# Third last gate-and-up selection made one down product sooner; token tiles of the last down products take turns over the banks

## The reference, cut to what matters

```python
xn = layernorm(x)                                   # 2048 tokens x 512
x = x + attn(xn, qkv, o_proj, gamma, beta) + ffn(xn, w_gate, w_up, w_down)

def ffn(x, w_gate, w_up, w_down):                   # hidden width 2048
    h = silu(x @ w_gate) * (x @ w_up)
    g = h.reshape(B, S, I // 4, 4)                  # of each four neighbours
    _, idx = top_k(abs(g), 2)                       # the two largest stay
    h_sparse = (g * mask(idx)).reshape(B, S, I)
    return h_sparse @ w_down
```

## Time and profile before

| | |
|---|---|
| median of 3 runs | 839.53 us |
| the profiled execution, its own time | 840.95 us |
| its span, first to last instruction | 839.2 us |
| TensorE busy, 3635 matmuls | 813.9 us, 97% |
| VectorE busy | 578.6 us, 69% |
| ScalarE busy | 314.1 us, 37% |
| mean granted TensorE clock | 0.992 |

### The profile page before, as it was taken

The page is one execution under the profiler, slowest core; times in us unless marked ns, Lnnn a source line. Parts: engine busy times, 40 slices in busy tenths (PEclk is TensorE's granted clock), DMA queues, the critical chain, the costliest instruction groups (busy, mean ns, idle before and its releaser), DMA issues.

```text
span 839.2 us, 9524 instructions
## 1 busy us (share of the span) xinstructions
PE 813.9 (97%) x3635; PEld 664.7 (79%) x3635; DVE 578.6 (69%) x985; ACT 314.1 (37%) x514; POOL 13.3 (2%) x33
## 2 busy tenths in 40 slices
PE   7998999999999999999999999998999999999997
PEld 5786887888888888887788788787888888888875
DVE  6856675445623347869988889699559568567796
ACT  5524133111511125554527436264234233323531
POOL 2100100000000000000000000000000000000000
PEclk9999999999999999999999999999999999999999
DMA  9511341240110208366534544871557262151002
GB/s 331 174 73 64 125 139 42 72 125 26 51 36 23 69 25 351 132 257 236 216 116 169 217 161 157 341 283 33 205 191 242 119 226 107 68 226 51 1 0 101
DMA packets 30012, 117.03 MB, mean 139 GB/s; under 512 B 2912, under 2 KB 2960, under 8 KB 27536
## 3 DMA queue, kind: packets, MB, share of 16 engines
q1 hardware_dynamic: 25792, 108.83, 35.0%
q10 hardware_dynamic: 4176, 7.60, 2.8%
HBM read 74.45 MB, written 41.97 MB: 139 GB/s over the span
## 4 chain that ended last, share of the span: by engine, by line
PE 72%; DVE 12%; ACT 5%; issue 3%; DVEq 0%
PE bank L481 10%; PE bank L483 10%; PE bank L482 9%; PE bank L605 9%; PE bank L607 9%; PE bank L606 9%; PE bank L687 5%; PE bank L689 5%; PE bank L688 5%; ACT mag L806 3%; PE bank L523 2%; DVE hs_lo L1153 1%; DVE wset L922 1%; DVE g_sum L1094 1%; ACT bank L802 1%
## 5 line engine op out<-in xcount | busy, mean ns | idle before, releaser
L605 PE MATMUL bank<-X_hi,wset 128*128 128x512 f32 x448 | 176.5, 394 | 3.5 <-DVE g_sum L1094 2.9
L606 PE MATMUL bank<-X_lo,wset 128*128 128x512 f32 x448 | 175.1, 391 | 0.0
L607 PE MATMUL bank<-X_hi,wset 128*128 128x512 f32 x448 | 175.1, 391 | 0.0
L605 PEld LDWEIGHTS bank<-X_hi,wset 128*128 128x128 f32 x448 | 84.5, 189 | 27.0 <-ACT bank L802 5.6
L607 PEld LDWEIGHTS bank<-X_hi,wset 128*128 128x128 f32 x448 | 84.4, 188 | 17.6
L606 PEld LDWEIGHTS bank<-X_lo,wset 128*128 128x128 f32 x448 | 84.5, 189 | 17.1
L687 PE MATMUL bank<-dw,hs_hi 128*128 128x512 f32 x224 | 87.9, 392 | 2.1 <-DVE acc L1118 1.6
L688 PE MATMUL bank<-dw,hs_hi 128*128 128x512 f32 x224 | 87.2, 389 | 0.0
L689 PE MATMUL bank<-dw,hs_lo 128*128 128x512 f32 x224 | 87.2, 389 | 0.0
L1118 DVE TENSOR_TENSOR acc<-bank,acc 128x512 f32<-128x512 f32 x64 | 43.4, 687 | 51.5 <-PE bank L689 51.5
L481 PE MATMUL bank<-xT_hi,zg_hi 128*128 128x512 f32 (+3 forms) x160 | 59.4, 371 | 0.1
(11 more groups left out here) (165 smaller groups left out, 1409.9 us busy)
## 6 DMA issues: line engine op xcount, KB each, us to landing
w_operands<-wset SPq DMA_DIRECT2D x8, 3584.0 KB, 11.8
wset<-w_operands SPq DMA_DIRECT2D x8, 3584.0 KB, 11.9
wsum<-w_units SPq DMA_DIRECT2D x28, 256.0 KB, 3.6
dw_raw<-L_ffn_w_down SPq DMA_DIRECT2D x14, 512.0 KB, 4.9
xw<-L_attn_x SPq DMA_DIRECT2D x4, 1024.0 KB, 9.6
xt_raw<-x_t SPq DMA_DIRECT2D x8, 512.0 KB, 7.2
xn_t<-xt_raw SPq DMA_DIRECT2D x8, 512.0 KB, 5.1
X_raw<-xn_t SPq DMA_DIRECT2D x8, 512.0 KB, 4.9
```

The source lines that it names most:

```text
L605: pe.matmul(dst[:], u[:, 0, :], x_hi, start=(first and kt == 0), stop=False, skip_group_check=True)
L606: pe.matmul(dst[:], u[:, 0, :], x_lo, start=False, stop=False, skip_group_check=True)
L607: last = pe.matmul(dst[:], u[:, 1, :], x_hi, start=False, stop=(kt == 1), skip_group_check=True)
```

## The change

It does four things.

1. Half 13 is selected in step 14, behind the selection of half 12, with its magnitudes in memory of its own (`mag_apart`, 144 KB, inside `wset0`, so after `gate_up(14)`). VectorE's comparisons and keeps for it stand between the four `add_down` of half 12. ScalarE makes its high parts in step 15, ahead of the last `down_hi` (conversion of down weights) and of two magnitudes of half 14.
2. Down products 13 and 14 add up in the same banks (6, 7, 2, 3); both belong to the same output tiles. `add_down(13)` is gone: four VectorE adds fewer. Half 15 takes banks (0, 1, 4, 5).
3. Down product 14 goes through r outside and the four token tiles inside; down product 15 does so for tiles (0, 1), then (2, 3).
4. On VectorE nothing stands any longer between the low parts of half 14 and the comparisons of half 15. The last gate and up sums are added ahead of the selection of half 14, and the last multiplication stands inside it. The remaining eight adds all come last.

The core of the diff:

```diff
+        mag_apart = at("mag_apart", 144 * KB, [P, G, W], F32)
-            return mag if i < ND - 2 else last_mag[i - (ND - 2)]
+            return mag if i < ND - 3 else mag_apart if i == ND - 3 else last_mag[i - (ND - 2)]
-            return bank[((6, 7, 2, 3), (0, 1, 4, 5), (6, 7, 2, 3))[i - (ND - 3)][t] ...
+            return bank[((6, 7, 2, 3), (6, 7, 2, 3), (0, 1, 4, 5))[i - (ND - 3)][t] ...
 # TensorE
+                pe.matmul(dst, s_hi, d_h, start=(r == 0 and i != ND - 2), stop=False)
+            def down_by_hidden(i, some):
+                for t in some:
+                    bank_free(i, t)
+                for r in range(G):
+                    if 0 in some:
+                        hidden_wait(i, r)
+                    for t in some:
+                        down_part(i, t, r)
+                if 2 <= n < N_Q:
+                    down(n - 2)
+                elif n == N_Q:
+                    down_by_hidden(ND - 2, range(TC))
+                elif n > N_Q:
+                    down_by_hidden(ND - 1, (0, 1))
+                    down_by_hidden(ND - 1, (2, 3))
 # ScalarE, step 15 behind the snapshots of P6
                 elif n == N_Q - 1:
+                    kept_hi(i)
                     down_hi(ND // 2 - 1)
+                    magnitude(ND - 2, 0)
+                    magnitude(ND - 2, 1)
 # ScalarE, end of step 14
+                if n == N_Q - 2:
+                    act.wait_ge(full[1], FILLS * (n + 1))
+                    for r in range(G):
+                        magnitude(ND - 3, r)
 # VectorE, end of step 14
+                elif n == N_Q - 2:
+                    add_down(i, 0)
+                    first_beats(i + 1)
+                    last_beats(i + 1)
+                    add_down(i, 1)
+                    count_beats(i + 1)
+                    add_down(i, 2)
+                    keep(i + 1, 0)
+                    keep(i + 1, 1)
+                    add_down(i, 3)
+                    keep(i + 1, 2)
+                    keep(i + 1, 3)
```

More of the change, by code:

```diff
@@ L306, in down_bank, with added_no @@
         def down_bank(i, t):
-            return bank[((6, 7, 2, 3), (0, 1, 4, 5), (6, 7, 2, 3))[i - (ND - 3)][t] if i >= ND - 3 else 6 + (TC * i + t) % 2]
+            return bank[((6, 7, 2, 3), (6, 7, 2, 3), (0, 1, 4, 5))[i - (ND - 3)][t] if i >= ND - 3 else 6 + (TC * i + t) % 2]
+        def added_no(i, t):
+            return TC * (i if i < ND - 2 else i - 1) + t + 1
         def a_free(n):
@@ L438, in _ @@
                         tile = (down_half[d] % 2) * TC + t
-                        sp.wait_ge(added, TC * d + t + 1)
+                        sp.wait_ge(added, added_no(d, t))
                         sp.dma_start(out_tiles[(d // NQ) * 2 * TC + tile], acc[:, tile, :]).then_inc(out_stored, 16)
@@ L665, in bank_free @@
                         pe.wait_ge(hid_ready, 4 * last + 1)
-                elif i == ND - 2:
+                elif i == ND - 1:
                     if t == 0:
@@ L672, in bank_free, with down_part, hidden_wait @@
                         pe.wait_ge(summed[t - 2], 2 * last + 2)
-                else:
-                    pe.wait_ge(added, TC * (ND - 3) + t + 1)
+            def down_part(i, t, r):
+                s_hi, s_lo = hs_hi_at(i)[:, r, t * P:(t + 1) * P], hs_lo_at(i)[r][:, t * P:(t + 1) * P]
+                d_h, d_l = dw_at(i // 2)[:, r // 2, 0, r % 2, :], dw_at(i // 2)[:, r // 2, 1, r % 2, :]
+                dst = down_bank(i, t)[:]
+                pe.matmul(dst, s_hi, d_h, start=(r == 0 and i != ND - 2), stop=False)
+                pe.matmul(dst, s_hi, d_l, start=False, stop=False)
+                last = pe.matmul(dst, s_lo, d_h, start=False, stop=(r == G - 1 and i != ND - 3))
+                if r == G - 1:
+                    last.then_inc(down_full, 1)
+            def hidden_wait(i, r):
+                pe.wait_ge(hs_ready, G * i + r + 1)
+                if i % 2 == 0 and r % 2 == 0:
+                    pe.wait_ge(dw_ready, i + r // 2 + 1)
             def down(i):
@@ L678, in down @@
                     bank_free(i, t)
-                    dst = down_bank(i, t)[:]
                     for r in range(G):
                         if t == 0:
[L682 to L690, removed]
+                            hidden_wait(i, r)
[5 more added lines that the diff above has]
+                    if 0 in some:
+                        hidden_wait(i, r)
+                    for t in some:
+                        down_part(i, t, r)
             for n in range(N_Q + 2):
@@ L808, in kept_hi @@
             def kept_hi(i):
+                if i == ND - 3:
+                    act.wait_ge(down_full, TC * i)
                 for r in range(G):
@@ L834, in _ @@
                 else:
-                    if i >= 0:
+                    if i >= 0 and n < N_Q - 1:
                         magnitudes(i)
@@ L866, in _ @@
                 nc.scalar.activation(g_sum[3][:], bank[0][:], ACT.Silu).then_inc(silu_ready, 1)
-                if n < N_Q - 1:
-                    last_silu(n)
+                if n == N_Q - 1:
+                    act.wait_ge(hid_ready, 4 * n + 2)
+                    magnitude(ND - 2, 3)
+                    act.wait_ge(hid_ready, 4 * n + 3)
+                    magnitude(ND - 2, 2)
+                last_silu(n)
                 if n == 2:
@@ L885, in _ @@
                 magnitude(ND - 1, r)
-            kept_hi(ND - 2)
-            last_silu(N_Q - 1)
             act.wait_ge(hid_ready, 4 * N_Q)
             magnitude(ND - 1, G - 1)
+            kept_hi(ND - 2)
             kept_hi(ND - 1)
@@ L1114, in add_down @@
                     dve.wait_ge(acc_loaded, 16 * (i // NQ + 1))
-                if i == ND - 2:
-                    dve.wait_ge(added, no - TC + 1)
                 dve.wait_ge(down_full, no + 1)
@@ L1163, in _ @@
                 i = n - 2
-                picks = i >= 0
+                picks = 0 <= i < ND - 3
                 if picks:
@@ L1184, in _ @@
                 elif n == N_Q - 1:
+                    for r in range(G):
+                        kept_lo(i, r)
                     down_lo(ND // 2 - 1)
@@ L1236, in _, with keep_all @@
                     add_down(i, 3)
-                elif picks and n < N_Q - 1:
+                elif n == N_Q - 2:
[10 more added lines that the diff above has]
+                    keep(i + 1, 3)
+                elif picks:
                     for t in range(TC):
                         add_down(i, t)
-            i = ND - 3
+            def keep_all(i):
+                keep(i, 0)
+                for r in range(1, G):
+                    keep(i, r)
+                    kept_lo(i, r - 1)
+                kept_lo(i, G - 1)
+            n, i = N_Q - 1, ND - 2
+            add_sum(0, n, bank[4], F_P4, g_sum[1], 3)
+            add_sum(1, n, bank[5], F_P4, a_tile(n, 1), 3)
+            first_beats(i)
+            last_beats(i)
+            hidden(n, 4, 2, g_sum[1], a_tile(n, 1))
+            count_beats(i)
+            keep_all(i)
+            dve.wait_ge(picked, G * (i + 1))
             first_beats(i + 1)
@@ L1245, in _ @@
             count_beats(i + 1)
[L1246 to L1268, removed]
+            keep_all(i + 1)
+            for i in (ND - 2, ND - 1):
+                for t in range(TC):
+                    add_down(i, t)
 INPUTS = ["L0_attn_x", "x_t", "L0_attn_qkv", "L0_attn_o_proj", "L0_attn_gamma", "L0_attn_beta",
```

9 lines of the change are left out of this document (removed).

## The result

The changed kernel takes 834.82 us (median of 8 runs, 834.42 to 836.92), the kernel before 839.42 us (8 runs, 838.1 to 841.58). The ratio is 0.9946, 95% interval 0.9933 to 0.9958: 4.6 us faster. The forecast was 835.6, range 834.1 to 838.4.

The account below looks back on a forecast made before the run. TensorE bounds the kernel, losing 5.87 us at the end, mostly waiting for VectorE's low parts and at low clock. New losses of 1.70 replace these: 4.17 gained, less 0.25, gives 3.9 us and 835.6 us, range 834.1 to 838.4.

Parts of the forecast that it names:

- (a): Step 14, bank 7: TensorE waits for VectorE's add of token tile 1, behind four comparisons; loss 0.65 us.
- (b): Step 15, first copies: the wait behind four magnitudes on ScalarE goes; gain 0.34 us.
- (c): Step 15, P5 copy: new instructions ahead of it on ScalarE make TensorE wait; loss 1.06 us.
- (d): From gate_up(15)'s end to product 15: product 14 without a gap, half 15's first low part slightly late; 0.33 us lost.
- (e): Clock at the new stalls (0.5, 0.9, 0.2 us): too short to bring the low clock, no cost.
- (f): Taking turns over banks in the last products: cost taken as 0, bounds 0 to 0.3 us.
- The rival on turns: Products 14 and 15: turns over four banks bring the clock down, making the kernel slower, up to 845 us; chance 0.06.
- (g): Kernel's end: last products of half 15 fill 0.68 us apart, so stores crowd; cost 0.25 us, bounds 0 to 0.4.
- the 3.19: VectorE work from 810.84 to 814.03, five instructions between the last two selections, leaving the path: 3.19 us.

Follow-up runs that it names:

- e6: Changed kernel with five VectorE additions (3.0 us) put between the low parts of half 14 and the comparisons of half 15; tail 72.25 us against 67.81.
- e2: Changed kernel with VectorE's add of token tile 1 in step 14 behind two comparisons of half 13, not four; tail 67.14 us against 67.81, median 835.66 us.
- e1: Changed kernel with ScalarE's two magnitudes of half 14 behind the P5 copies in step 15, not ahead; tail 66.71 us against 67.81, median 835.53 us.
- e5: Kernel before with only the turns over token tiles in products 14 and 15 put in; tail 72.98 us against 72.1.

## Why the prediction was right

*What bounds.* That 5.87 us were lost in the tail, and that they hung on the path VectorE - low part - TensorE, held: with three microseconds of VectorE's work put back between the selections (e6), TensorE idled 2.93 us ahead of product 15, the low clock was back, and the tail was 4.44 longer. That it came to 72.25, near the 72.1 of the kernel before, is in part chance: e6 has the new waits, the turns and the shared banks, which that kernel has not.

*(a), (b), (c).* 0.67, 0 and 1.07 us measured for 0.65, 0 and 1.06. e2 and e1 remove (a) and (c) by moving the one or two instructions that the prediction named, and give back 0.67 and 1.10.

*(d).* Half 15's comparisons were to begin 811.86 - 798.69 = 13.17 us after gate_up(15), and began 13.05 after it. The wait and restart ahead of product 15 were 0.21 instead of 0.33.

*(e), (f).* No low clock after waits of 0.34 and 0.74 us. In products 13 and 14 there is no late start at all: 21.76 us from 796.55, 0.2267 apart with turns over four banks as without (the 0.08 us ahead of product 15, at 818.39, are in (d)). The rival on turns finds nothing here. The rule of the Trainium skill that was set beside it (TensorE: Matmul & The Clock Gate, section "A second HAM failure mode: psum-queue depth-cycling") tells of a kernel that idled between its groups of matmuls; this one cycles through banks without idling, and the granted clock is 1.00 from 796 to 830 us.

*(g), the term that was off.* The end was to cost 0.25 us more and cost 0.07 less. Two stores 0.68 us apart landed in 2.0 us each; the 2.4 of the earlier trace rows was of the last two of five stores in a row, each 0.6 us behind the other, which landed in 2.1 us (the first) to 2.5 us (the last). With 0.12 from (d), that is the difference between 3.9 and 4.3 us. The rest of the 4.6 between the medians is scatter: the repeat gave 2.7 (839.3 against 836.61). So it is partly luck that the median, too, came within 0.8 us of the forecast.

*What it did not see.* It gave the shared banks no term of their own, though 1.1 us of the 4.3 are theirs (the two adds were counted inside the 3.19). And it took the turns as independent of where the last sums stand, which e5 refuted. In the change itself neither matters, because all parts are there.

## What to carry to other kernels

At a kernel's end, count what stands on the engine between two results that the bound engine needs, and take out whatever no one waits for; where the idle time also brings the low clock, it costs half as much again (4.4 us for 3.0 in e6). Before putting instructions ahead of another in a queue, add up the queue from its last fixed event to the one that the bound engine waits for: six more instructions here overran it by one microsecond, and moving two cured it. An interleaved order asks for all its buffers at its start, so free them first.

## What the hardware showed that was not expected

Waits of TensorE of 2.1 us, at three places of the kernel, were followed by the low clock in 27 of 41 cases and by full clock in 14; in step 8 this moved the execution by 1.4 us each time. Waits of 1.6 to 1.9 us never were (24 cases), and two of four waits of 2.9 us were not either. Compare versions of such a kernel by the stretch that the edit touches, which repeated to 0.04 us, when their times scatter by 3.
